# GpSimd's multiply ahead of its accumulating transfer in every unit of a state-space scan

## The reference, cut to what matters

```
def step(hst, inp):
    dt_t, B_t, C_t, x_t = inp
    dA = jnp.exp(dt_t[:, :, None] * A)
    hst = hst * dA + (dt_t * x_t)[:, :, None] * B_t[:, None, :]
    y = jnp.einsum('bds,bs->bd', hst, C_t)
    return (hst, y)
```

## Time and profile before

| | us |
|---|---|
| median of three runs | 3439.36 |
| the profiled execution, first to last instruction (span) | 3433.5 |
| layer 1, from the first multiply L1517 to the end of the span | 2091.8 |
| VectorE busy | 2457.5 (72%) |
| TensorE busy | 2862.0 (83%) |
| GpSimd busy | 1818.2 (53%) |
| ScalarE busy | 1597.8 (47%) |

### The profile page before, as it was taken

One profiled execution on the slowest core, in us unless ns is written; L12 is line 12 of the kernel. 1 busy time (PEld: TensorE's weight loads), 2 busy tenths in 40 slices (PEclk: granted clock), 3 DMA queues, 4 the chain that ended last, 5 costly groups with the idle time before them and its releaser, 6 DMA issues.

```text
span 3433.5 us, 37791 instructions
## 1 busy us (share of the span) xinstructions
PE 2862.0 (83%) x11066; PEld 1598.6 (47%) x11066; DVE 2457.5 (72%) x3184; ACT 1597.8 (47%) x2252; POOL 1818.2 (53%) x771
## 2 busy tenths in 40 slices
PE   7999999999999987687877887887877877887774
PEld 3545454554545443345445445445445444444442
DVE  3444444444444244999999998999999999999992
ACT  1122122222212215576676675676675675676550
POOL 0121111112111112778689689689688689689791
PEclk9999999999999997787997987987987987988877
DMA  5002020110202222332353353354353353353362
GB/s 189 6 25 80 0 79 31 48 59 21 79 0 80 86 70 71 67 73 67 76 117 94 77 121 91 77 117 93 77 121 90 77 124 88 81 125 89 88 135 62
DMA packets 193931, 270.53 MB, mean 79 GB/s; under 512 B 16877, under 2 KB 82545, under 8 KB 193738
## 3 DMA queue, kind: packets, MB, share of 16 engines
q1 hardware_dynamic: 146152, 183.53, 16.7%
q0 software_dynamic: 44032, 83.91, 13.9%
q10 hardware_dynamic: 3554, 0.88, 0.1%
HBM read 167.32 MB, written 42.22 MB: 61 GB/s over the span
## 4 chain that ended last, share of the span: by engine, by line
DVE 26%; issue 15%; PE 7%; POOL 5%; ACT 4%; DMA 4%; DVEq 1%; POOLq 0%; SPq 0%; ACTq 0%
DVE hs L1640 13%; DVE acc L1681 8%; POOL hs L1517 3%; PE bank L1210 2%; DMA fin<-y_rows,idx_first 2%; DVE xm L1608 2%; PE bank L1153 1%; ACT bank L1395 1%; DVEq L110 1%; POOL acc L1536 1%; PE bank L1183 1%; DMA b_wide<-b_rows 1%; PE bank L1177 1%; DMA out<-fin 1%; PE bank L1236 1%
## 5 line engine op out<-in xcount | busy, mean ns | idle before, releaser
L1517 POOL TENSOR_TENSOR hs<-u,b_wide 128x2048 f32<-128x2048 f32 x256 | 1280.7, 5026 | 75.4 <-DVE u L1632 75.2
L1640 DVE TENSOR_TENSOR_SCAN hs<-bank,hs 128x512 f32<-128x512 f32 x1024 | 1229.5, 1213 | 29.1 <-POOL hs L1517 16.5
L1210 PE MATMUL bank<-ident,hs 128*128 128x128 f32 x4096 | 750.3, 319 | 358.2 <-DVE hs L1640 237.4
L1395 ACT ACTIVATE bank<-dt,decay 128x512 f32<-128x512 f32 x1024 | 697.9, 689 | 622.6 <-DVE hs L1640 621.0
L1210 PEld LDWEIGHTS bank<-ident,hs 128*128 128x128 f32 x4096 | 560.9, 163 | 892.3 <-issue 525.9
L1681 DVE SCALAR_TENSOR_TENSOR acc<-bank,c_t,acc 128x512 f32<-128x512 f32 x800 | 585.4, 732 | 91.1 <-PE bank L1210 80.9
L1153 PE MATMUL bank<-h_t,w_in 128*128 128x512 f32 x1024 | 547.6, 622 | 9.7 <-ACT h_t L1326 5.4
L1536 POOL DMA_DIRECT2D acc<-scaled x224 | 254.3, 1135 | 321.9 <-ACT scaled L1402 298.9
L1236 PE MATMUL bank<-w_y,zs 128*128 128x512 f32 x512 | 260.2, 599 | 3.5 <-DVE fin L1698 2.5
L726 POOL TENSOR_TENSOR y_rs<-y_var,mhalf 128x8 f32<-128x8 f32 x8 | 16.0, 2002 | 440.4 <-DVE y_var L200 440.4
L585 PE MATMUL bank<-z_t,w_k 128*128 128x512 f32 x512 | 221.8, 594 | 5.8 <-ACT z_t L682 5.8
(11 more groups left out here) (154 smaller groups left out, 3079.2 us busy)
## 6 DMA issues: line engine op xcount, KB each, us to landing
acc<-scaled POOLq DMA_DIRECT2D x224, 256.0 KB, 4.1
w_in<-in_L_cond_W_in SPq DMA_DIRECT2D x128, 256.0 KB, 4.0
b_wide<-b_rows SPq DMA_DIRECT2D x128, 256.0 KB, 3.7
z<-in_x SPq DMA_DIRECT2D x8, 2048.0 KB, 8.3
res<-in_x SPq DMA_DIRECT2D x8, 2048.0 KB, 8.3
x_rows<-res SPq DMA_DIRECT2D x7, 2048.0 KB, 7.4
fin<-x_rows SPq DMA_DIRECT2D x56, 256.0 KB, 2.8
out<-fin SPq DMA_DIRECT2D x56, 256.0 KB, 2.0
```

What stands on the lines that cost most here:

```text
L1210: last = nc.tensor.transpose(state_banks[n % len(state_banks)][:, j * P:(j + 1) * P], hs[:, q % RING, j, t * P:(t + 1) * P], ident[:, :])
L1395: nc.scalar.activation(decay_bank(k)[:, :], dt[:, par, j, :], ACT.Exp, scale=g.decay[:, j, s:s + 1]).then_inc(da_ready, 1)
L1517: nc.gpsimd.tensor_tensor(hs[:, q % RING, :, :], u[:, 4 * half:4 * half + 4, :], b_wide[:, s % 2, :].unsqueeze(1).to_broadcast([P, 4, CHUNK]),
L1640: nc.vector.tensor_tensor_scan(block, decay_bank(k)[:, :], block, 0.0, ALU.mult, ALU.add).then_inc(scanned, 1)
```

## The change

In each unit of a turn GpSimd first multiplies the inputs of unit q, and then issues the accumulating transfer of unit q - 4. Before, it was the other way round.

```
             def turn(b, par, prev, more):
                 for q in range(HALVES):
+                    inputs(b, q)
                     if q >= RING:
                         pool_state(b, q - RING)
-                    inputs(b, q)
                     if more and q >= HALVES - 2:
                         dt_x(b + 1, 1 - par, q - (HALVES - 2))
```

## The result

The changed kernel takes **3498.3 us** (median of 4 runs, 3494.08 to 3501.74), the kernel before 3438.36 beside it (4 runs, 3436.74 to 3440.71). The ratio is 1.0171, with a 95% interval from 1.0158 to 1.0184: 59.9 us slower, where 20 were forecast and 3470 was the end of the range. The profiled execution's span is 3499.9 us against 3433.5, so 66.4 us are to be found. As a run that execution took 3501.74 us, only 1.8 more than its span. So most of the 5.9 us that separate span and median of the kernel before come from their being different executions.

The account below looks back on a forecast made before the run. GpSimd was taken to bound each batch from unit 24 on, VectorE pacing earlier stretches with TensorE and ScalarE. The terms 5 x 3.0 + 3.5 + 1.3 = 19.8 us on 3439.4 gave 3459 us, range 3443 to 3470.

Parts of the forecast that it names:

- The multiply, units 4 to 23: GpSimd's multiply in units 4 to 23 comes 2 to 8 us earlier, nobody waits for it: 0.
- The last transfer: Unit 27's transfer, issued behind unit 31's multiply, lands later: +3.0 us in b = 2 to 6, +3.5 b = 1, +1.3 b = 0.
- b = 7: Last batch, without a next batch's load: landing 3346.3, add at 3352.20, so 0.
- The estimate of 3.9: Landing of the last transfer beside the `b_wide` load by the DMA page: 3.3 + 0.6 us; total about +13.
- The other end of the bound, 3.3: Last transfer's landing time in us if nothing else moves; total then 9 us, 3448.
- The head start: From unit 23 to unit 31, every GpSimd multiply is 2.6 us sooner, 2.1 in b = 1.
- ScalarE's scaling: Scaling two units after a transfer, saturated stretch: could stand 2.2 us late with a 6.6 us landing; taken as 0.
- the three rivals: Whole kernel: faster, 3424 us, chance 0.09; within 0.2%, 3444, chance 0.13; slower still, 3472 to 3475, chance 0.12.
- slower still: Units 25 to 29: ScalarE's scaling waits for slow transfers, 13 us on top, 3472 to 3475 us; chance 0.12.

Follow-up runs that it names:

- both edits: Changed kernel with the shift product (L273) behind block 14 and, in units 30 and 31, the transfer ahead of the multiply again: 3405.7 us, ratio 0.9913.

## Why the prediction was wrong

Right in sign, wrong in size: 20 us forecast, 59.9 measured.

- **The failed step** is "The multiply, units 4 to 23 ... comes 2 to 8 us earlier. Nobody waits for it there: 0." The first half held. The second asked only who waits for the multiply by a semaphore. Nobody does; but a VectorE product that needs nothing of the multiply (the root that it reads was done 5.4 us earlier) is held while the multiply runs. The term is 31.3 us by unit 3, all of it the product's 7 x (5.06 - 0.59), and was set at 0. *SBUF — State Buffer* of the Trainium skill, section "Who interferes with whom", states that VectorE and GpSimd share one pair of ports as an exclusive lock, taken by VectorE instructions with two SBUF inputs and by those in a two-port mode, and that the one who is late blocks for the whole instruction. By that rule the trace agrees: 0.59, 0.73, 1.71, 2.50 and 5.05 us for the same 128x4 product, each to the end of a multiply.
- The evidence was in the trace of before. L273 took 0.59 us there while the 128x4 instruction of L267 took 0.17 beside an idle GpSimd, and its end fell on a multiply's end to 0.02 us. Read with that question, "where does the multiply of unit 6 go?" has an answer: from 2673.85 to right behind unit 5's, on top of L273.
- **The last transfer**: right. Forecast +3.0 for b = 2 to 6, +3.5 for b = 1, +1.3 for b = 0, 19.8 in all; measured 21.8 in units 29 to 31 and 20.7 with the product out of the way. By batch the growth is 1.8, 3.7, 3.4, 2.9, 4.1, 3.4 and 2.5 us for b = 0 to 6. The wait for unit 26's landing, a third of it by place (7.2 in unit 29), was not in the account. The landing of 4.9 us, taken from one row at another place, came out at 4.9, and the 3.5 with the load held back shows that the load is what makes the difference. In the changed kernel itself the same transfer of b = 7, with no load beside it, lands 3.2 us after its multiply. The estimate of 3.9 from *DMA: Bandwidth & Descriptors* of the Trainium skill is not borne out; the measurement decides. The other end of the bound, 3.3, is what the held load nearly gives.
- **The head start** of 2.6 us: right. From the first scan of unit 24 to the end of unit 31's multiply, the mean of b = 1 to 6 is 53.5 us before and 50.9 after, 2.0 less in b = 1 (forecast 2.1) and 2.0 to 3.4 less in the others. With both edits unit 30 is shorter than before by 1.2 us in b = 3 to 6, and one of two stalls goes.
- **ScalarE's scaling**, taken as 0: VectorE's stall ends with the landing, and ScalarE waits for those landings only 5.8 us in 8 places. The term was small, as taken.
- **Unit 19**: not foreseen at all. Each fall of the granted clock there costs 2.9 us; in the traced executions the change moved the count from 4 to 6 (5.3 us), other edits to 1, 2 or 7. The count is of one execution each: the four runs with the old order in units 30 and 31 have mean granted clocks of 0.897 to 0.908 and times of 3462.49 down to 3450.03 us. What tips it is open: TensorE's unit 18 is the same to 0.01 us in both cases above, and no run here was made for it. It also means that differences of 10 to 15 us between these kernels can't be laid on an edit without looking at unit 19.
- **b = 7**, taken as 0: b = 7 and the end grew by 3.4 us. No wait for the landing of unit 26's or 27's transfer is among them. The changed order with the product on GpSimd, which has the same order in b = 7, takes 291.2 us there, no more than before, so the order is not shown to cost anything in b = 7.

None of the three rivals is what happened. The nearest in time, "slower still", rested on a scaling that waits, and of its 13 us at most these 5.8 occurred.

## What to carry to other kernels

When a change makes one engine's long instructions start sooner, list not only who waits for them but also which small instructions of the engine that shares its memory ports now fall beside them: here 4 elements a partition cost 5 us. Idle time of GpSimd can be what keeps VectorE's small SBUF-to-SBUF instructions short, so give these a place in the queue from which the end of a GpSimd instruction comes soon, or put them on GpSimd itself. The place must be ahead of that end: behind block 14 the product started 0.7 us before it and lasted 0.73 us, behind block 15 it started 0.4 us after it, the next multiply followed at once, and the product lasted 5.05 us. And an order that is worth nothing in the middle of a loop can be worth something of either sign at its end, so price the last iterations by themselves and give them their own order.

## What the runs showed of the hardware that was not expected

- A VectorE instruction of 128x4 with one SBUF tensor operand and a constant waits for GpSimd's multiply just as one with two operands does (2.75 us, to within 0.04 us of the multiply's end), while 128x512 scans and adds with one operand in PSUM run beside it unchanged at 1.21 and 0.73 us.
- Who comes first is not to be read from the records to a tenth of a microsecond: in the changed kernel L273's record starts at 2442.48, the multiply's at 2442.68, and it is VectorE that waits.
- Two transfers of 256 KB started 0.2 us apart: the first lands 4.9 us after it could be issued, and 3.5 us when the other is held back.
- The granted clock fell at the start of unit 19 in 1, 2, 4, 6 or 7 of seven batches, in one traced execution of each kernel, though all give TensorE the same instructions there.
